# A four-layer attention block on one core: the row scaling of the probabilities moves from VectorE to GpSimd

## What is computed

```
attn = softmax(Q K^T)            # 1024 x 1024 per image, rows sum to one
out  = attn V                    # L1 and L3: also group norm before, output product folded into V
x    = x + out
```

## Time and profile before

| | |
|---|---|
| time, median of 3 runs | 1603.95 us (1603.63 to 1605.78) |
| span of the profiled execution | 1601.4 us, 2.5 us below the median of the runs |
| PE matmul busy | 1359.2 us, 85% |
| VectorE busy | 1013.7 us, 63% |
| ScalarE busy | 586.2 us, 37% |
| GpSimd busy | 123.3 us, 8% |

### The profile page before, as it was taken

How to read it: one execution, slowest core, us unless ns; L and a number is a source line. 1 busy time by engine, 2 the same in 40 slices (tenths; PEclk the granted TensorE clock), 3 DMA queues, 4 the chain that set the end, 5 groups by cost and what they waited for, 6 DMA issues and landing times.

```text
span 1601.4 us, 21756 instructions
## 1 busy us (share of the span) xinstructions
PE 1359.2 (85%) x7584; PEld 1024.8 (64%) x7584; DVE 1013.7 (63%) x1837; ACT 586.2 (37%) x797; POOL 123.3 (8%) x314
## 2 busy tenths in 40 slices
PE   4789888859988989876988898896798798889689
PEld 3668654448776865445877776444687687545577
DVE  3656578666565657765646566776565565696655
ACT  3424234524332423533433332353343242245243
POOL 0000011210000002110000000222000000112100
PEclk8799979969978988987998997997898899899799
DMA  4000110000000020000000003000000001200000
GB/s 137 0 27 1 40 41 2 1 1 1 29 1 27 1 67 14 1 1 1 1 29 1 27 0 80 2 1 1 1 0 29 0 1 27 54 1 2 1 1 27
DMA packets 16396, 27.24 MB, mean 17 GB/s; under 512 B 2576, under 2 KB 6800, under 8 KB 16272
## 3 DMA queue, kind: packets, MB, share of 16 engines
q1 hardware_dynamic: 16272, 25.66, 5.8%
HBM read 8.61 MB, written 4.19 MB: 8 GB/s over the span
## 4 chain that ended last, share of the span: by engine, by line
issue 88%; POOL 7%; PE 4%; POOLq 0%; DVE 0%; ACT 0%
PE ring L584 4%; POOL cprobs L555 3%; POOL rstd L539 2%; POOL idle_pool L554 2%; PE ring L654 0%; PE ring L710 0%; POOLq L424 0%; POOLq L538 0%; PE ring L715 0%; ACT h_hi L944 0%; DVE y L1136 0%; POOLq L542 0%; DVE gn_nb L1202 0%; DVE gn_sc L1200 0%; DVE gn_msc L1201 0%
## 5 line engine op out<-in xcount | busy, mean ns | idle before, releaser
L1002 ACT ACTIVATE cprobs<-ring 128x1024 f32<-128x1024 f32 (+1 forms) x192 | 152.1, 812 | 204.8 <-PE ring L830 204.2
L584 PE MATMUL ring<-probsT_hi,vt_hi 128*128 128x512 f32 x384 | 157.3, 410 | 13.6 <-DVE probsT_lo L1086 13.6
L890 ACT ACTIVATE probsT_hi<-ring 128x1024 fp32r<-128x1024 f32 x96 | 98.0, 1026 | 182.1 <-PE ring L654 181.7
L1086 DVE TENSOR_TENSOR probsT_lo<-ring,probsT_hi 128x1024 fp32r<-128x1024 f32 x96 | 116.5, 1221 | 66.2 <-ACT probsT_hi L890 66.2
L806 PE MATMUL ring<-ks,qs 96*128 96x512 f32 (+3 forms) x384 | 144.0, 452 | 14.2 <-DVE part_max L1331 6.1
L584 PE MATMUL ring<-probsT_hi,vt_lo 128*128 128x512 f32 x384 | 153.1, 399 | 0.0
L584 PE MATMUL ring<-probsT_lo,vt_hi 128*128 128x512 f32 x384 | 152.6, 397 | 0.0
L1331 DVE TENSOR_REDUCE part_max<-ring 128x2 f32<-128x1024 f32 (+3 forms) x128 | 127.3, 1017 | 36.1 <-PE ring L810 17.9
L1119 DVE TENSOR_REDUCE neg_max<-ring 128x1 f32<-128x1024 f32 x96 | 116.8, 1221 | 32.7 <-PE ring L584 29.1
L830 PE MATMUL ring<-qs,ks 98*128 98x512 f32 (+3 forms) x384 | 115.0, 394 | 14.7 <-DVE part_max L1331 12.2
L539 POOL TENSOR_TENSOR rstd<-var_eps,half_neg 128x2 f32<-128x2 f32 (+1 forms) x52 | 46.2, 889 | 1026.7 <-DVE var_eps L1197 555.9
(11 more groups left out here) (218 smaller groups left out, 2670.7 us busy)
## 6 DMA issues: line engine op xcount, KB each, us to landing
qs<-q_hi SPq DMA_DIRECT2D x64, 128.0 KB, 2.3
xin<-x_dram SPq DMA_DIRECT2D x4, 1024.0 KB, 4.9
qs<-q_lo SPq DMA_DIRECT2D x32, 128.0 KB, 2.3
out_dram<-y SPq DMA_DIRECT2D x8, 512.0 KB, 3.1
qs<-max_rows SPq DMA_DIRECT2D x64, 4.0 KB
raw_L_wv<-L_wv_dram SPq DMA_DIRECT2D x2, 256.0 KB, 6.1
raw_L_woT<-L_woT_dram SPq DMA_DIRECT2D x2, 256.0 KB, 6.3
raw_L_wqT<-L_wqT_dram SPq DMA_DIRECT2D x2, 256.0 KB, 6.6
```

The lines of the kernel that those rows point to most:

```text
L584: ins = mm(out, w, m, start=first and n == 0, stop=last and n == len(every) - 1)
L890: A(dst, flat(name) if src is None else src, ACT.Identity, bias=bias, scale=scale).then_inc(hi_ready, 1)
L1002: A(causal_probs(step, two, n), slot(event_name(e))[:, :, 0:n], ACT.Exp).then_inc(act_read, 1)
L1086: ins = v.tensor_tensor(dst, src, f32(hi), ALU.subtract)
```

## The change

The multiplication of the 96 tiles leaves VectorE's program and stands in GpSimd's. VectorE keeps the reciprocal, and its semaphore (`row_inv_ready`) now tells GpSimd. GpSimd first runs a multiplication of one column that nobody reads (`idle_scale`), then the scaling in place, whose semaphore `probs_scaled` PE waits for as before. The wait of VectorE for its own reciprocal is gone.

```diff
-DVE_STEPS = 101
+DVE_STEPS = 77
...
+        idle_scale = sb("idle_scale", [P, NT])
...
+        row_inv_ready = sem("row_inv_ready")
...
+            def scale_rows(b, l):
+                for ti in range(NT):
+                    pool.wait_ge(row_inv_ready, b * (3 * NT) + FULL_NO[l] * NT + ti + 1)
+                    pool.tensor_tensor(idle_scale[:, ti:ti + 1], half_neg[:, 0:1], half_neg[:, 0:1], ALU.mult)
+                    pool.tensor_scalar(probs[:, ti % 2, :], probs[:, ti % 2, :], row_inv[:, ti:ti + 1], None,
+                                       ALU.mult).then_inc(probs_scaled, 1)
+
             with pool.Fori(0, B) as b:
-                for name in norms[:3]:
+                scale_rows(b, "L0")
+                root(b, norms[0])
+                scale_rows(b, "L1")
+                for name in norms[1:3]:
                     root(b, name)
...
                 root(b, norms[-1])
+                scale_rows(b, "L3")
...
                 def scale(ti):
                     wait_read(dve, b, f"{l}.s{ti}")
-                    then(b, v.reciprocal(row_inv[:, ti:ti + 1], row_sum[:, ti:ti + 1]))
-                    v.tensor_scalar(probs[:, ti % 2, :], probs[:, ti % 2, :], row_inv[:, ti:ti + 1],
-                                    None, ALU.mult).then_inc(probs_scaled, 1)
+                    v.reciprocal(row_inv[:, ti:ti + 1], row_sum[:, ti:ti + 1]).then_inc(row_inv_ready, 1)
```

## The result

The changed kernel takes 1662.1 us (median of 4 runs, 1657.9 to 1666.8); the kernel before took 1604.9 us beside it (4 runs, 1603.6 to 1611.4). The ratio is 1.037, with a 95% interval of 1.033 to 1.041. The change costs 57 us, where no change was forecast. The profiled execution spans 1662.4 us, 61 us more than the one of before.

What follows compares the result with a forecast made beforehand. PE, busy 85%, bounds L1 and L3; L0 is limited almost equally by VectorE's work and four-engine latency. Terms: +3.1 (L1, L3) - 1.7 (L0) = +1.4 us, forecast 1605 us, no change; range 1600.5 to 1620.

Steps and rivals of the forecast that it cites:

- the price of one scaling on GpSimd: Cost of one 1024-column scaling on GpSimd, taken as 1.07 us from the masking row, bounds 0.88 and 1.64 us.
- The bound above: Upper bound on one scaling: all 0.41 us of a 256-column masking as per-column cost, giving 1.64 us.
- slow rival: GpSimd is slow per column, 1.64 us or so per scaling: +15.5 us in sum, 1619; chance 0.30.
- the spare time of 0.8 us or more covers what is left: L1 and L3, tiles between the stalling ones: earlier reciprocal and spare time cover the 0.49 us longer path.
- The stall at tile 1: In L1 and L3: transposes come 0.26 us later; 8 stalls, plus 4 at L3's tile 7, 3.1 us lost.
- The sum for L0: L0's four batches: -1.19, +0.29, -0.5 and -0.3 us, in all -1.7 us.
- head term: At the head of each L0 batch, 0.69 us gained on v1's wait, since vt_lo follows a bare reciprocal.
- Contention: GpSimd's scaling beside VectorE's remaining full-attention instructions costs nothing; the rival, low part held back, gives 1613, chance 0.06.
- What would make it wrong: Signs: scaling 1.2 us or more, PE idle behind probs well beyond 20 us, other tiles waiting, L0 low parts late.

Runs made afterwards that it cites:

- masking run: Changed kernel with GpSimd's multiplication replaced by an always-true 1024-column masking, rows unscaled: 1587.8 us, ratio 0.991 to the kernel before; again 1590.4 us, 0.994.
- split tiles: Changed kernel with each tile scaled in two parts, 768 columns on VectorE and 256 on GpSimd: 1597.0 us, one run.

## Why the prediction was wrong

**The step that failed** is the price of one scaling on GpSimd: "I take 1.07, because the masking too reads and writes each column once and does more to it than a multiplication". It took 2.85 us. The bound above, 1.64, failed as well. Both came from one other operation. The masking run shows that the extrapolation over columns was sound (1.04 measured) and that the step from one operation to another was not. On the same data the forms differ by a factor of 2.7.

**The slow rival** had the right sign and mechanism and the wrong size. With 2.85 us its own sum gives -1.7 + 8 x 1.78 + 4 x 1.85 = 20 in L0, where the profiled execution has 22, and 12 x 2.04 = 24.5 in L1 and L3, where it has 44. So the second step that failed, had the price been right, is the sentence that at the tiles between "the spare time of 0.8 us or more covers what is left". It holds for a path 0.49 us longer and not for one 2.3 us longer. In VectorE's order the reciprocal of tile 3 stands behind the row maximum of tile 4, and that waits for PE's scores (549.12, 550.26 above). Between those scores and the transposes of tile 3 PE has about as much other work as before, while the way through GpSimd got 2.3 us longer. The exponential of tile 3 was done by 548.5 and held nothing up. These waits at tiles 3 and 6 are 10 us of what is missing; the rest is PE's own work, which took longer, most of it in L3 at the lower granted clock; no term had that.

**The stall at tile 1** in L1 and L3 was placed rightly. From the first row maximum to tile 1's transposes there are 14.64 us before (510.80 to 525.44) and 16.71 after (528.50 to 545.21): 2.07 us more, and the prediction's steps give 2.04 for 2.85 us. Moving the reciprocal took the stall at tile 1 away.

**The sum for L0** was wrong by about 2 us in three of four batches even at the price that it assumed (masking run, second batch: 49.88 against 51.81 us, forecast 0.29 longer). In these the granted clock rose, from 0.80 to 0.86 in the second; in the first it did not, and the sum held to 0.2 us. The steps moved instructions along a fixed clock. What raised the clock is open.

**The wait for `vt_lo`** ahead of v1 fell from 15.0 to 12.0 us in four batches, as the head term of 0.69 us each said. **Contention** was rightly costed at nothing: 29 of VectorE's 96 low parts `probsT_lo` lay wholly inside a scaling on GpSimd and took 1.22 us on average, those that met none as well. What does contend is VectorE's own scaling, as the split tiles show, and it had left. **What would make it wrong** named the right signs, a scaling above 1.2 us and more than 20 us of idle time behind it.

What stays open is why L2 takes 188.6 or 192.5 us or more with the same instructions. The granted clock in it differs, 0.89 to 0.83, but its mean does not order the times: 189.0 us came at 0.86 and 192.5 at 0.88. What sets it off was not found.

## What to carry to other kernels

The price of an operation on GpSimd is to be measured for that very form before work is moved there; a row of another operation gives the cost of columns for that operation only, and bounds drawn from it are no bounds. Spare time in front of an instruction is good for the lengthening that it was measured against and no more: once a path grows by more than the spare time of a tile, that tile stalls too, so a rival with a higher price needs its own list of stalls. An idle engine is not a free one: what it takes over gets its latency. Here taking 67 us of work from VectorE lost 3.7%, where moving two of its instructions forward gave 1.2%, of which about 8 us lie where the moves act and most of the rest in a layer that nobody touched.

## What the runs showed of the hardware that was not expected

- GpSimd on 128 x 1024 float32 in SBUF: masking 1.04 us, product with a column as second tensor input 1.89, tensor by constant 2.77, tensor by column as scalar 2.85. A one-input form was slower than the two-input one.
- VectorE's multiplication of 128 x 1024 by a constant took 0.69 us, by a column 0.75.
- VectorE's multiplication from SBUF to SBUF (768 columns, 0.62 us) held GpSimd's instructions up: a one-column instruction on GpSimd took 0.62 us in place of 0.19 in 82 tiles, and 256 columns took 1.24 us in place of 0.92 in 14. VectorE's low parts, with one input in SBUF and one in PSUM, were not disturbed.
- The constant on VectorE, 0.06 us less a tile, came with a kernel 0.4 to 1.0% faster, at least 6.9 us, where 96 x 0.06 is 5.8 us at the very most. In its profiled execution L0 is 3.7 us shorter over four batches and L2 2.8 us. So a small edit can be worth more than the time that it saves in its own instructions, and a difference of some 0.5% in this kernel need not come from the edit's own mechanism.
